# Packing the context loads of a gated cross-attention and MoE kernel, and queueing its input loads without waits

## The reference, cut to what matters

```python
# x (8, 112, 256), ctx (8, 375, 256); 8 experts, w1 (8, 1024, 256), w2 (8, 256, 1024)
def _L0_xattn_ref(x, w1, w2):                       # called with w1 = w2 = ctx
    h = jnp.einsum('eth,efh->etf', x, w1)
    g = jax.nn.gelu(h, approximate=True)
    return jnp.einsum('etf,efh->eth', g, w2)

def _L0_ffn_ref(x, gate_w, gate_b, w1, b1, w2, b2):
    top1 = jnp.argmax(xf @ gate_w.T + gate_b, axis=-1)
    for e in range(n_experts):
        y = jax.nn.relu(xf @ w1[e].T + b1[e]) @ w2[e].T + b2[e]
        out = out + jnp.where((top1 == e)[:, None], y, 0)

x = x + jnp.tanh(g_xattn[0]) * _L0_xattn_ref(_layernorm(x), ctx_1024, ctx_1024)
x = x + jnp.tanh(g_ffn[0]) * _L0_ffn_ref(_layernorm(x), gate_w, gate_b, w1, b1, w2, b2)
```

## Time and profile before

| | us |
|---|---|
| median of three runs | 135.09 |
| span of the profiled execution, first to last instruction | 134.5 |
| TensorE busy with matmuls | 112.0 |
| VectorE busy | 53.8 |
| ScalarE busy | 28.7 |
| GpSimd busy | 32.9 |
| mean DMA rate over the span | 209 GB/s |
| mean granted TensorE clock | 0.934 of full speed |

### The profile page before, as it was taken

One profiled execution on the slowest core, in us unless ns is written; L12 is line 12 of the kernel. 1 busy time (PEld: TensorE's weight loads), 2 busy tenths in 40 slices (PEclk: granted clock), 3 DMA queues, 4 the chain that ended last, 5 costly groups with the idle time before them and its releaser, 6 DMA issues.

```text
span 134.5 us, 2238 instructions
## 1 busy us (share of the span) xinstructions
PE 112.0 (83%) x742; PEld 101.2 (75%) x743; DVE 53.8 (40%) x210; ACT 28.7 (21%) x82; POOL 32.9 (24%) x70
## 2 busy tenths in 40 slices
PE   5955992996874868999599986999999999999930
PEld 5855881895773747999499966999998989999810
DVE  0505032766447042557489621424232324232210
ACT  4620220321321130243024301313040313111000
POOL 7404021434122001202752247002020202020220
PEclk9996589689999777799999999999999999999999
DMA  4856766375688999574339999999999200000010
GB/s 92 229 145 176 191 178 209 123 204 157 201 214 264 256 313 410 199 241 171 82 96 376 388 383 409 344 421 422 417 392 422 105 4 29 1 5 34 5 41 24
DMA packets 9644, 28.14 MB, mean 209 GB/s; under 512 B 1125, under 2 KB 5919, under 8 KB 7456
## 3 DMA queue, kind: packets, MB, share of 16 engines
q1 hardware_dynamic: 7600, 24.89, 53.0%
q0 software_dynamic: 864, 2.12, 5.4%
q10 hardware_dynamic: 1168, 0.98, 2.5%
HBM read 26.13 MB, written 2.11 MB: 210 GB/s over the span
## 4 chain that ended last, share of the span: by engine, by line
PE 68%; DMA 17%; issue 8%; DVE 2%; SPq 1%; POOL 1%; POOLq 0%; DVEq 0%
PE bank L950 24%; PE bank L959 21%; DMA x<-in_x 8%; PE bank L877 8%; PE bank L864 6%; DMA region<-in_ctx_rows 6%; DMA region<-x_rows,from_row 3%; PE bank L895 2%; PE bank L924 2%; PE bank L886 2%; PE bank L937 1%; POOL out_rows L326 1%; PE bank L854 1%; PE bank L906 1%; SPq L219 1%
## 5 line engine op out<-in xcount | busy, mean ns | idle before, releaser
L950 PE MATMUL bank<-region,w 128*128 128x128 f32 x288 | 35.2, 277 | 1.7 <-issue 1.7
L950 PEld LDWEIGHTS bank<-region,w 128*128 128x128 f32 x288 | 33.8, 192 | 2.6 <-issue 2.1
L959 PE MATMUL bank<-w,region 128*128 128x256 f32 x144 | 32.6, 379 | 0.0
L959 PEld LDWEIGHTS bank<-w,region 128*128 128x128 f32 x144 | 26.7, 190 | 3.3
L437 ACT ACTIVATE region<-bank,smalls 128x128 f32<-128x128 f32 x40 | 12.5, 363 | 42.4 <-PE bank L950 42.4
L864 PE MATMUL bank<-xnT,region 128*125 128x112 f32 x96 | 14.7, 312 | 7.9 <-issue 4.9
L864 PEld LDWEIGHTS bank<-xnT,region 128*125 128x125 f32 x96 | 13.5, 223 | 8.9 <-issue 8.9
L326 POOL DMA_INDIRECT out_rows<-region,to_row x9 | 8.9, 990 | 41.2 <-DVE region L769 40.6
L877 PE MATMUL bank<-region,w 125*112 125x256 f32 x48 | 15.9, 482 | 1.6 <-issue 1.6
L753 DVE TENSOR_SCALAR region<-bank,smalls 128x128 f32<-128x128 f32 x32 | 9.6, 345 | 15.5 <-PE bank L950 14.9
L321 POOL DMA_INDIRECT region<-x_rows,from_row x9 | 9.3, 1029 | 16.8 <-issue 10.8
(11 more groups left out here) (115 smaller groups left out, 92.9 us busy)
## 6 DMA issues: line engine op xcount, KB each, us to landing
w<-in_w1t SPq DMA_DIRECT2D x8, 1024.0 KB
w<-in_w2t SPq DMA_DIRECT2D x8, 1024.0 KB
region<-in_ctx_cols SPq DMA_DIRECT2D x8, 375.0 KB, 6.9
region<-in_ctx_rows SPq DMA_DIRECT2D x8, 375.0 KB
b2b<-in_b SPq DMA_DIRECT2D x1, 1024.0 KB, 18.3
x_rows<-x ACTq DMA_DIRECT2D x8, 113.8 KB, 5.3
x<-in_x SPq DMA_DIRECT2D x1, 448.0 KB, 11.3
x<-in_x SPq DMA_DIRECT2D x2, 112.0 KB, 2.3
```

Of the source, the lines that this page charges most:

```text
L950: mm = pe.matmul(hT_ps[k][:, part % 2 * P:(part % 2 + 1) * P], w1[:, e, n * H + part * P:n * H + (part + 1) * P], xgT[:, j % 2, n * P:(n + ...
L959: mm = pe.matmul(y[:, 0:D], hidT[:, q, part, :], w2[:, e, part * D:(part + 1) * D], start=(part == 0), stop=(part == KH - 1))
```

## The change

The two context arrays become one, packed by batch: for each of 128 partitions the columns (750 numbers) and then the rows (768 numbers; the last three partitions are zeros). So a batch is one load of 759 KB in pieces of 6072 bytes, except batch 0, which still takes two, columns and rows. Each batch and each expert gets semaphores of its own, and SyncE issues everything up to expert 5 without a wait. The columns of batch 0 are issued ahead of batch 1's x, and the x of batches 4 to 7 behind batch 2's context. Only experts 6 and 7 still wait, for the data that lie in their place. In TensorE's stream `scores(b)` now waits for the whole of batch b (the columns alone for b = 0), and `attend` waits for context only at b = 0.

```diff
-        cxT = region[:, 0:B * KD * CTX].rearrange("p (b n) -> p b n", b=B)
-        cx = region[:, B * KD * CTX:].rearrange("p (b n) -> p b n", b=B)
+        cxs = region[:, :].rearrange("p (b n) -> p b n", b=B)
+        cxT, cx = cxs[:, :, 0:KD * CTX], cxs[:, :, KD * CTX:CW]
...
-            def load_context(b, q):
-                sp.dma_start(cxT[:, b, :], ctx_cols[b]).then_inc(cxT_in[q], 16)
-                sp.dma_start(cx[0:CR, b, :].rearrange("p (c d) -> p c d", c=CC),
-                             ctx_rows[b].rearrange("(c p) d -> p c d", p=CR)).then_inc(cx_in[q], 16)
+            def load_context(b):
+                sp.dma_start(cxs[:, b, :], ctx[b]).then_inc(cx_in[b], 16)
...
             load_x(0, 1).then_inc(x_in[0], 16)
+            sp.dma_start(cxT[:, 0, :], ctx[0, :, 0:KD * CTX]).then_inc(cxT0_in, 16)
             load_x(1, 1).then_inc(x_in[1], 16)
-            load_context(0, 0)
+            sp.dma_start(cx[:, 0, :], ctx[0, :, KD * CTX:CW]).then_inc(cx_in[0], 16)
             load_x(2, 2).then_inc(x_in[2], 16)
-            load_context(1, 1)
-            sp.wait_ge(cxT_in[0], 16)
-            sp.wait_ge(cx_in[0], 16)
-            load_context(2, 0)
+            load_context(1)
+            load_context(2)
             load_x(4, 4).then_inc(x_in[3], 16)
-            sp.wait_ge(cxT_in[1], 16)
-            sp.wait_ge(cx_in[1], 16)
-            load_context(3, 1)
-            with sp.Fori(2, B // 2) as t:
-                for q in range(2):
-                    sp.wait_ge(cxT_in[q], 16 * t)
-                    sp.wait_ge(cx_in[q], 16 * t)
-                    load_context(2 * t + q, q)
-
-            load_expert(0, 0)
+            for b in range(3, B):
+                load_context(b)
+
+            load_expert(0)
             sp.dma_start(b2b[:], b2.partition_broadcast(P)).then_inc(b2_in, 16)
-            sp.dma_start(w1[:, 1, :], w1t[1]).then_inc(w1_in[1], 16)
-
-            sp.wait_ge(xn2T_ok, B)
-            sp.wait_ge(w1_in[0], 16)
-            sp.dma_start(w1[:, 2, :], w1t[2]).then_inc(w1_in[0], 16)
-            for q in range(2):
-                sp.wait_ge(first_in[q], 16)
-            sp.wait_ge(xg_in[0], 16)
+            for e in range(1, E - 2):
+                load_expert(e)
+
+            sp.wait_ge(xnT_done, B)
             sp.wait_ge(xgT_done, 1)
             sp.wait_ge(xn2T_done, B)
...
+            for e in range(E - 2, E):
+                load_expert(e)
...
             def scores(b):
                 pe.wait_ge(xnT_ok, b + 1)
-                pe.wait_ge(cxT_in[b % 2], 16 * (b // 2 + 1))
+                pe.wait_ge(cx_in[b] if b else cxT0_in, 16)
...
             def attend(b):
                 pe.wait_ge(gel_ok, b + 1)
-                pe.wait_ge(cx_in[b % 2], 16 * (b // 2 + 1))
+                if b == 0:
+                    pe.wait_ge(cx_in[b], 16)
```

More of the change, by code:

```diff
@@ L35 @@
 CC, CR = 3, CTX // 3
+CW = KD * CTX + CC * D
 ROW = D + 4
@@ L47, with gated_cross_attention_moe @@
 NOWHERE = 65536.0
-def gated_cross_attention_moe(nc, x, ctx_rows, ctx_cols, small, w1t, w2t, b2, out):
+def gated_cross_attention_moe(nc, x, ctx, small, w1t, w2t, b2, out):
     x2_dram = nc.dram_tensor("x2_rows", (TOKENS, ROW), F32, kind="Internal").ap()
@@ L70, in gated_cross_attention_moe @@
         tg = sb("tg", [P, 2])
-        region = sb("region", [P, B * (KD * CTX + CC * D)])
-        cxT = region[:, 0:B * KD * CTX].rearrange("p (b n) -> p b n", b=B)
-        cx = region[:, B * KD * CTX:].rearrange("p (b n) -> p b n", b=B)
+        region = sb("region", [P, B * CW])
+        cxs = region[:, :].rearrange("p (b n) -> p b n", b=B)
+        cxT, cx = cxs[:, :, 0:KD * CTX], cxs[:, :, KD * CTX:CW]
         hid = region[:, 0:2 * H].rearrange("p (q n) -> p q n", q=2)
@@ L163, in gated_cross_attention_moe @@
         small_in, b2_in = sem("small_in"), sem("b2_in")
[L164 to L167, removed]
+        cxT0_in = sem("cxT0_in")
+        cx_in = [sem(f"cx_in{b}") for b in range(B)]
+        w1_in = [sem(f"w1_in{e}") for e in range(E)]
+        w2_in = [sem(f"w2_in{e}") for e in range(E)]
         pool_step = sem("pool_step")
@@ L208, in _, with load_expert @@
         def _(sp):
-            def load_context(b, q):
-                sp.dma_start(cxT[:, b, :], ctx_cols[b]).then_inc(cxT_in[q], 16)
-                sp.dma_start(cx[0:CR, b, :].rearrange("p (c d) -> p c d", c=CC),
-                             ctx_rows[b].rearrange("(c p) d -> p c d", p=CR)).then_inc(cx_in[q], 16)
-            def load_expert(e, q):
-                sp.dma_start(w1[:, e, :], w1t[e]).then_inc(w1_in[q], 16)
-                sp.dma_start(w2[:, e, :], w2t[e]).then_inc(w2_in[q], 16)
+            def load_context(b):
+                sp.dma_start(cxs[:, b, :], ctx[b]).then_inc(cx_in[b], 16)
+            def load_expert(e):
+                sp.dma_start(w1[:, e, :], w1t[e]).then_inc(w1_in[e], 16)
+                sp.dma_start(w2[:, e, :], w2t[e]).then_inc(w2_in[e], 16)
             def load_x(b, n):
@@ L943, in up @@
                 pe.wait_ge(xgT_ok, j + 1)
-                pe.wait_ge(w1_in[e % 2], 16 * (e // 2 + 1))
+                pe.wait_ge(w1_in[e], 16)
                 for part in parts:
@@ L1042, in _ @@
                 turn_block(e + 2, e % 2)
-                pe.wait_ge(w2_in[e % 2], 16 * (e // 2 + 1))
+                pe.wait_ge(w2_in[e], 16)
                 pe.wait_ge(o_ok, e)
@@ L1074, in _ @@
                 turn_block(BLOCKS, 1)
-            pe.wait_ge(w2_in[1], 16 * E // 2)
+            pe.wait_ge(w2_in[E - 1], 16)
             pe.wait_ge(o_ok, E - 1)
@@ L1121 @@
         "x": np.ascontiguousarray(x).reshape(TOKENS, D),
-        "ctx_rows": np.ascontiguousarray(ctx_1024),
-        "ctx_cols": np.ascontiguousarray(
-            np.asarray(ctx_1024).transpose(0, 2, 1).reshape(B, KD, P, CTX).transpose(0, 2, 1, 3)).reshape(B, P, KD * CTX),
+        "ctx": np.ascontiguousarray(np.concatenate([
+            np.asarray(ctx_1024).transpose(0, 2, 1).reshape(B, KD, P, CTX).transpose(0, 2, 1, 3).reshape(B, P, KD * CTX),
+            np.pad(np.asarray(ctx_1024).reshape(B, CC, CR, D).transpose(0, 2, 1, 3).reshape(B, CR, CC * D),
+                   ((0, 0), (0, P - CR), (0, 0)))], axis=2)),
         "small": np.ascontiguousarray(np.concatenate([
```

## The result

The changed kernel takes 123.75 us, the median of four runs (122.82 to 125.16), against 135.56 for the kernel before on the same chip. The ratio is 0.911, with a 95% interval of 0.902 to 0.920: faster, and 123 had been forecast. The profiled execution took 125.16 us and has a span of 123.4 us; TensorE is busy for 107.6 of it. Medians and ranges here are over all executions, while ratios leave out the slow ones, those more than 1.5% above the fastest of their kernel.

What follows compares the result with a forecast made beforehand. TensorE was taken as the bound (112.0 of 134.5 us busy), with holes from slow context loads and SyncE's waits. Gains of 21.3 less losses of 9.5 gave 122.7, plus 0.6 for the median: 123 us, 8-in-10 range 115.5 to 130.

Steps and rivals of the forecast that it cites:

- Attention, gain 18.7: Attention turns: context loads at 330 GB/s leave no holes before `scores`; attention ends at 34.2, not 52.91, gaining 18.7 us.
- allowance for VectorE in turn 5: Attention's turn 5: VectorE has routing work of its own there, allowed 0.5 us (0 to 2).
- `first_block` at full clock, 0.9: `first_block` after attention: its twelve matmuls, 2.55 us before, run at full clock, gaining 0.9 us.
- The store, cost 2.8: Last store of x after attention: lands in 8.6 us beside weights, so the first gather starts 2.8 us later.
- The gather, cost 4.2: First gather, before `turn_block(1)`: takes 7.9 us beside weight loads instead of 3.69, costing 4.2 us.
- VectorE's lag and the clock, 0.5 + 2.0: Behind the first gather: VectorE's second block and overflow table follow later, 0.5 us; TensorE returns at low clock, 2.0 us.
- The hole before `up(3)`, gain 1.7: Before `up(3)`: expert weights issued without a hold arrive in time, so the hole goes, gaining 1.7 us.
- The signs named beforehand: Loads, attention, gather, TensorE's pause and `up(3)`: trace signs of being right, such as over 300 GB/s from 3 us on.
- stuck behind the queue: Rival at stores and first gather: served only after loads queued ahead; 137 to 149 us, middle 141; chance 0.13.
- Free passage: Rival at stores and first gather: small transfers pass at once, none of the 9.5 us paid; 114 us; chance 0.25.
- Slow loads: Rival at context loads: rate stays at 175 GB/s, 135.4 us, or about 127 at 220 GB/s; chance 0.15.

Runs made afterwards that it cites:

- kernel with 56 transposes: The changed kernel with 56 dummy transposes in TensorE's wait for the first gather: 121.22 us, ratio 0.892.
- the two kernels on 125 partitions: The changed kernel with each batch's context in two loads, rows on 125 partitions, in 1 KB or 3 KB pieces: 138.72 and 139.77 us.
- the hold until blocks 1, 0 and 2 are in: The changed kernel, but weights from expert 3 on issued only when the gathers of blocks 1, 0 and 2 have landed: 116.91 us, ratio 0.853.
- base run: The changed kernel once more, unchanged, as base for others on the same chip: 123.34 us, ratio 0.897.

## Why the prediction was right, term by term

- **Attention, gain 18.7:** measured 52.91 - 36.56 = 16.4. The turns are the 3.36 forecast (3.36, 3.35, 3.35), the one with the rank matmuls 3.91. The loads came at 344 GB/s from 3 to 17 us, close to the 330 that I took, and at 415 behind that. The term was too large by 2.3 because of the start. Batch 1's x landed 4.04 us after its issue, where 2.3 had been, and TensorE paused 1.50 us for it in front of `turn_xn(0)`: `scores(0)` starts at 8.35, where 7.4 was forecast. Then the 24 matmuls of `scores(0)` and `scores(1)` took 4.86 us in the chain, little more than half of the speed of later ones. How much of this comes with the execution profiled, another one shows: in the kernel with 56 transposes, whose instructions are the same up to there, the matmuls of `scores(0)` run at full speed, `scores(0)` starts at 7.63 and attention ends at 35.05. So 1.5 of the 2.3 are not in every execution. That the pause makes these matmuls slow is not shown (see the last section). The allowance for VectorE in turn 5 (0.5) wasn't needed.
- **`first_block` at full clock, 0.9:** 2.55 to 1.34, 1.2. The prediction's own two rows (2.55 and 1.31) give 1.2 too, not the 0.9 that it wrote.
- **The store, cost 2.8:** it landed after 8.89 us, 8.6 had been taken, and the first gather starts 12.0 us after attention's end, not 10.1. With the 0.9 above that is 1.9 net, as forecast. The 2.3 us "in quiet" of the earlier trace rows was not the last store of the kernel before: that one, issued at 56.05, took 5.4 us and landed at 61.45, just ahead of the table of row numbers (61.78), so it was barely hidden.
- **The gather, cost 4.2:** 6.55 against 3.69, so 2.9. Here the 7.9, taken close to the nearest row (8.3, two transfers at once), was too high; the direction and the place were right.
- **VectorE's lag and the clock, 0.5 + 2.0:** `turn_block(1)` to `up(3)`, less the old hole of 1.73, went from 12.9 to 15.5, 2.5 as forecast; the 56 transposes put nearly all of it on the clock.
- **The hole before `up(3)`, gain 1.7:** gone.

The net in the trace is 134.5 - 123.4 = 11.1 against 11.8. Two terms were off by 2.3 and 1.3 in opposite directions, so the sum is better than its parts, and that is luck. So is a part of the last step: the prediction added 0.6 to the span to get a time, but in every execution listed with its span the time is 1.7 to 1.9 above it. The profile of the kernel before therefore belongs to an execution of some 136.3 us and not to one near 135. With 1.8 the sum would have given 124.5, against 123.75 measured.

The signs named beforehand all came: a share near 1 with over 300 GB/s, the turns, attention's end between 33 and 37, the gather between 6 and 9, the pause of over 5 with the low clock behind it, and no hole before `up(3)`.

Of the rivals, *stuck behind the queue* is out: the last store took 8.89 us, with some 6.5 MB of loads ahead of it (20.7 MB issued by then, less the 14.2 that 366 GB/s move in 38.8 us) and 4.2 MB more issued while it was under way. The seven stores before it took 6.4 to 8.2 us. That is no more than beside some 4 MB. *Free passage* is out for the same row. *Slow loads* did not happen in the changed kernel, but the two kernels on 125 partitions show what it would have been, and it was priced too low: 139 and 140, not 135. ScalarE's store issues took 0.31 to 0.52 us; nothing held them.

What the prediction did not see is how the gain is shared. It gave the rate to the partitions, as a reading of one share and one rule, and the runs bear this out. But it also named SyncE's waits as the cause of the holes, and counted the end of the hold on the weights as a gain of 1.7. Removing the waits gained nothing: on 125 partitions the kernel without them is 1.6% slower, and on 128 partitions the kernel with every old wait is 6 us faster than the changed one. The lowest time of the versions tried is that of the packed context with the hold until blocks 1, 0 and 2 are in, 116.91 us, ratio 0.853 (0.845 to 0.860); the kernel before with nothing but the padding, 0.861 (0.854 to 0.867), can't be told from it.

## What to carry to other kernels

Look at the DMA share while a load is the only thing under way: a share well under 1 with the queue full says that the load's shape, not the waits, limits it, and here padding the rows from 125 partitions to 128 was worth 14 us without the waits and 18 with them (135.99 to 117.61). A wait in the load queue can be protection: before it is removed, ask which small transfer on another queue ends on the critical path in that stretch, and hold bulk loads that are not needed yet until that one, and its successors, have landed. The hold has two ends: too short, and a later gather pays (9.1 us to land, 0.8 of it waited for by TensorE); too long, and a weight is late (2.0 us).

## What the runs showed that I had not expected

Three times as large pieces on 125 partitions (3 KB for 1 KB) left the rate at 192 GB/s to the digit, and on 128 partitions 1 KB pieces still ran at 338 to 384. Dummy transposes of one and the same tile ran at 112 to 116 ns each, where two transposes alone take 0.44 us; they are cheap filling, and many are needed to fill a wait.

At the start of the changed kernel 24 matmuls took 5.07 us on TensorE's timeline, while the granted clock of that stretch reads 1.00. In a second execution of the same kernel they took 3.79, and with 56 transposes later in the stream, twelve took 1.47 and the other twelve 1.53 (in this order: changed kernel, base run, 56 transposes):

```profile
8.35 5.07 PE L841 MATMUL bank<-xnT,region 128*125 128x112 f32 x24
```

```profile
8.14 3.79 PE L841 MATMUL bank<-xnT,region 128*125 128x112 f32 x24
```

```profile
7.63 1.47 PE L841 MATMUL bank<-xnT,region 128*125 128x112 f32 x12
10.07 1.53 PE L841 MATMUL bank<-xnT,region 128*125 128x112 f32 x12 [0.97 <-DMA region<-in_ctx]
```

The matmuls' own durations told of the slow start where the clock's column did not. The pause before them does not sort the cases: `scores(0)` ran at full speed behind a pause of 0.99 us (56 transposes) and slowly with none, 1.81 us for its twelve in the kernel before. Why it is slow in some executions stays open.
